# Index lists from six half-precision instructions, attention's last batch in halves, its row statistics in the first steps

## The chip, the cores and the metric

The kernel runs on one core of one Trainium2 chip. The metric is the device time of one launch in microseconds (us), as the median of three runs: 826.29 us before the change (824.8 to 826.83). The profiled execution, from which every row below is taken, was a run of its own and took 823.37 us.

## The reference

The reference takes hidden states x of shape [4, 512, 256] (2048 tokens of 256 values) and computes a macaron block in float32:

```
x = x + 0.5 * moe(layernorm(x))
x = x + attention(layernorm(x), w_qkv, w_o)      # 16 heads of 16, causal, softmax
x = x + 0.5 * moe(layernorm(x))
```

moe is a top-2 mixture of 8 experts with a capacity of C = 640 pairs per expert:

```
probs = softmax(x @ Wg); gate_vals, expert_idx = top_k(probs, 2)
pos   = how many earlier (token, choice) pairs went to the same expert
kept  = pos < C
dispatch_mask[expert, pos] = token                  # the index list
h = relu(x[dispatch_mask] @ w1[e]);  out[token] += gate * (h @ w2[e])
```

The index list is what the change is mostly about: for each expert and each of its 640 places, which token stands there.

## The kernel before, in words

The program has three stages, one after the other, each a block of its own in which the five engines run their own instruction streams and meet by semaphores: `feed_forward` with the tag first, `attention`, and `feed_forward` with the tag second. A block begins when every engine has left the block before it.

**feed_forward.** The 2048 tokens stand as 128 partitions by T = 16 columns. The first stage loads x, transposes it and computes the router's logits on TensorE; in the second stage attention has left logits and moments behind. VectorE then takes the two largest logits of each token, counts with a running sum, and TensorE adds over the partitions (L721, L722), so that each of the K * T = 32 columns of pairs has a position within its expert. The list is built as a sum of 32 outer products. Places are numbered as 128 lanes by LC = 40 tiles (8 experts by 5). For each pair column n, VectorE writes `of_tile[:, n, :]` (40 values: the token's number where the pair's tile is, else 0; L619) and `of_lane[:, n, :]` (128 values: 1 where the pair's lane is; L620), and TensorE adds the product of the two into ps_x (L733), waiting for each pair column by `lane_ready`. After every eighth product it runs 8 products whose result nobody reads (`spin`, L222), and 60 more after the last one. `spin` multiplies a table of ones; its only effect is that TensorE is not idle.

VectorE turns the sum into `gather_now` and `gather_index` (L624, L625). GpSimd waits for the normed rows and the shares to be stored in DRAM (`stored`, written by SyncE from `xn`, which ScalarE fills at L175, and `shares`), then gathers the 5 tiles of expert 0 and the 5 of expert 1 by indirect DMA (L410). TensorE transposes the gathered tiles in three batches of 2, 2 and 1 (L748, with 8 spins between), ScalarE and VectorE split them into a high and a low part (L501, L633, with the split of w2 at L548 between the first and second batch on VectorE), and the loop over the 8 experts begins with the matmul at L765.

GpSimd also fills the constant tables at the start of the first stage (`Constants.fill`, L91 to L95 by iota, `wide_gate` after them), and copies `slot_tile` into `slots` at the start of either stage (L381). VectorE waits for that copy (`slots_made`) before its routing work.

**attention.** Queries, keys and scores are worked in 16 units of 4 heads (4 units per batch). The order of all engines is one list, `PLAN`, made by `step_plan(v)` for v from -5: step v issues the batch work (`rows`, `stacks`, `values_in`), the scores of unit v + 2 (six pieces, S), the keys of unit v (six pieces, N), and so on. `normalize(b)` is in the plan four steps ahead of a batch; on VectorE it computes the row statistics of batch b (L1150 to L1155), on GpSimd the inverse root and the normed rows. Front pieces take turns in two pairs of PSUM banks: a piece waits for whoever reads the piece two before it, for scores VectorE's maximum (L1180). For the last batch, `project` adds the result to x in one instruction (L1218), `turn_x` transposes x (8 transposes, L1393) once `out_ready` is set, ScalarE copies the result (L1122), and `logits` multiplies by the gate (16 matmuls, L1401). At its start TensorE runs 70 spins.

## Time and profile before

| | us |
|---|---|
| median of three runs | 826.29 |
| lowest and highest | 824.8 and 826.83 |
| profiled execution | 823.37 |
| its span on the core | 821.6 |
| TensorE matmul busy in the span | 766.5 (93%) |
| VectorE busy | 434.2 (53%) |
| ScalarE busy | 376.2 (46%) |
| GpSimd busy | 316.8 (39%) |

The span runs from the first to the last instruction of the profile; 1.77 us of the profiled execution lie around it. Busy time of TensorE includes spins, so 93% is not 93% of useful work. The granted clock is the share of full speed (2.4 GHz) at which TensorE was let run; it has the two levels 1.0 (2.4 GHz) and 0.5 (1.2 GHz), and a value between them is a stretch with both. The stages lie at 0 to 294 us (first), 294.7 to 545.7 us (attention) and 545.98 us to the end (second).

### The profile page before, as it was taken

The page shows a single profiled execution, that of the slowest core. Times are in us where ns is not written, and L with a number is a line of the kernel's source. Part 1 is how long each engine was busy: PE and PEld are TensorE (multiplying, and loading weights), DVE is VectorE, ACT ScalarE, POOL GpSimd, SP SyncE. Part 2 cuts the span into 40 slices and gives each one's busy share as a digit, 9 for nine tenths or more (in the row PEclk, how much of TensorE's full clock was granted, in tenths as well). Part 3 has the DMA queues.
Part 4 walks back from the last instruction along what each step waited for, and adds up shares of the span by engine and source line. Part 5 has one row for each costly group of instructions (what it writes and reads, how often), then busy time and mean ns, then how long its engine had stood idle before and what let it go on. Part 6 is the DMA issues. An engine that isn't in the chain of part 4 may idle for free. (4 is left out here: it accounts for less than half of the span.)

```text
span 821.6 us, 16019 instructions
## 1 busy us (share of the span) xinstructions
PE 766.5 (93%) x6176; PEld 675.1 (82%) x6176; DVE 434.2 (53%) x850; ACT 376.2 (46%) x630; POOL 316.8 (39%) x373
## 2 busy tenths in 40 slices
PE   9689999999999987898998989967899999999997
PEld 5579999999999975565665655655899999999997
DVE  5945445534634226767676675456446345444630
ACT  4415545634544301556646556513345445544631
POOL 6073454464424263232232122222644554463133
PEclk9779999999999997899999999986999999999999
DMA  9542553354242154201222010024541553454122
GB/s 305 160 147 74 146 141 93 87 155 126 47 121 27 16 166 154 76 18 72 78 81 106 33 70 11 26 78 126 182 128 41 155 134 82 107 146 117 26 27 25
DMA packets 61862, 80.27 MB, mean 98 GB/s; under 512 B 10916, under 2 KB 48804, under 8 KB 61812
## 3 DMA queue, kind: packets, MB, share of 16 engines
q1 hardware_dynamic: 46452, 60.34, 21.8%
q0 software_dynamic: 15360, 19.23, 12.8%
q8 instruction: 35, 0.57, 0.3%
q14 instruction: 15, 0.12, 0.0%
HBM read 49.62 MB, written 19.01 MB: 84 GB/s over the span
## 5 line engine op out<-in xcount | busy, mean ns | idle before, releaser
L655 DVE SCALAR_TENSOR_TENSOR second_h_lo<-second_ps_h,second_h_hi 128x320 fp32r<-128x320 f32 x128 | 63.0, 492 | 105.2 <-ACT second_h_hi L514 105.2
L655 DVE SCALAR_TENSOR_TENSOR first_h_lo<-first_ps_h,first_h_hi 128x320 fp32r<-128x320 f32 x128 | 62.9, 492 | 104.8 <-ACT first_h_hi L514 104.8
L418 POOL DMA_INDIRECT after_first<-first_scaled,first_add_now x40 | 69.4, 1736 | 117.5 <-ACT first_scaled L507 110.9
L418 POOL DMA_INDIRECT out_dram<-second_scaled,second_add_now x40 | 69.0, 1725 | 117.2 <-ACT second_scaled L507 111.5
L1180 DVE TENSOR_REDUCE at_maxima<-at_ps_front 128x4 f32<-128x512 f32 (+2 forms) x96 | 97.0, 1040 | 21.1 <-PE at_ps_front L1321 20.6
L1052 POOL TENSOR_SCALAR_AFFINE_SELECT at_probs<-at_probs 128x512 f32<-128x512 f32 x64 | 41.3, 658 | 147.0 <-ACT at_probs L1110 147.0
L776 PE MATMUL second_ps_o<-second_w_hi,second_h_hi 128*128 128x256 f32 x320 | 90.9, 284 | 0.0
L776 PE MATMUL first_ps_o<-first_w_hi,first_h_hi 128*128 128x256 f32 x320 | 90.7, 283 | 0.0
L776 PE MATMUL second_ps_o<-second_w_lo,second_h_hi 128*128 128x256 f32 x320 | 89.7, 280 | 0.0
L776 PE MATMUL second_ps_o<-second_w_hi,second_h_lo 128*128 128x256 f32 x320 | 89.7, 280 | 0.0
L776 PE MATMUL first_ps_o<-first_w_lo,first_h_hi 128*128 128x256 f32 x320 | 89.5, 280 | 0.0
L776 PE MATMUL first_ps_o<-first_w_hi,first_h_lo 128*128 128x256 f32 x320 | 89.5, 280 | 0.0
L1110 ACT ACTIVATE at_probs<-at_ps_keys 128x768 f32<-128x768 f32 (+1 forms) x96 | 81.1, 879 | 17.5 <-PE at_ps_keys L1352 17.0
L514 ACT ACTIVATE second_h_hi<-second_ps_h 128x320 fp32r<-128x320 f32 x128 | 56.1, 438 | 60.4 <-PE second_ps_h L765 60.4
L514 ACT ACTIVATE first_h_hi<-first_ps_h 128x320 fp32r<-128x320 f32 x128 | 56.1, 438 | 60.4 <-PE first_ps_h L765 60.4
L765 PE MATMUL first_ps_h<-first_xt_hi,first_w_hi 128*128 128x320 f32 x256 | 59.0, 312 | 2.2 <-DVE first_xt_lo L633 2.2
L776 PEld LDWEIGHTS second_ps_o<-second_w_hi,second_h_lo 128*128 128x128 f32 x320 | 60.9, 190 | 0.0
L776 PEld LDWEIGHTS first_ps_o<-first_w_lo,first_h_hi 128*128 128x128 f32 x320 | 60.8, 190 | 0.0
L776 PEld LDWEIGHTS second_ps_o<-second_w_lo,second_h_hi 128*128 128x128 f32 x320 | 60.8, 190 | 0.0
L776 PEld LDWEIGHTS second_ps_o<-second_w_hi,second_h_hi 128*128 128x128 f32 x320 | 60.7, 190 | 0.0
L776 PEld LDWEIGHTS first_ps_o<-first_w_hi,first_h_hi 128*128 128x128 f32 x320 | 60.7, 190 | 0.0
L776 PEld LDWEIGHTS first_ps_o<-first_w_hi,first_h_lo 128*128 128x128 f32 x320 | 60.7, 190 | 0.0
(297 smaller groups left out, 1763.5 us busy)
## 6 DMA issues: line engine op xcount, KB each, us to landing
first_w_raw<-in_L_ffn_w_dram SPq DMA_DIRECT2D x16, 1024.0 KB, 8.9
second_w_raw<-in_L_ffn_w_dram SPq DMA_DIRECT2D x15, 1024.0 KB, 5.7
at_q_stack<-at_pre_hi SPq DMA_DIRECT2D x12, 256.0 KB, 2.5
at_k_stack<-at_pre_hi SPq DMA_DIRECT2D x12, 256.0 KB, 2.6
x<-_attn_hidden_states_dram SPq DMA_DIRECT2D x4, 512.0 KB, 5.4
after_first<-x SPq DMA_DIRECT2D x4, 512.0 KB, 7.8
normed_rows<-first_xn SPq DMA_DIRECT2D x4, 512.0 KB, 4.6
x<-after_first SPq DMA_DIRECT2D x4, 512.0 KB, 5.6
```

Of the source, the lines that this page charges most:

```text
L418: pool.indirect_dma_start(sum_rows, bass.IndirectOffsetOnAxis(ap=add_now[par][:, s:s + 1], axis=0), scaled[par][:, s, :], None, bounds_che ...
L514: act.activation(h_hi[:, f, a * HALF:(a + 1) * HALF], ps_h[:, f % 2, a, 0:HALF], ACT.Relu).then_inc(h_hi_done, 1)
L655: v.scalar_tensor_tensor(h_lo[:, f, a * HALF:(a + 1) * HALF], ps_h[:, f % 2, a, 0:HALF], 0.0, h_hi[:, f, a * HALF:(a + 1) * HALF].bitcast( ...
L765: last = pe.matmul(ps_h[:, f % 2, a, 0:HALF], w, m, start=(n == 0), stop=(n == len(parts) - 1))
L776: last = pe.matmul(ps_o[:, (par + s) % 2, 0:D], h[:, f, cs], w[par][:, f, :], start=(f == 0 and n == 0), stop=(f == FT - 1 and n == 2))
L1052: pool.affine_select(block_of, block_of, [[0, GROUP], [1, P]], ALU.is_ge, 0.0, base=0, channel_multiplier=-1).then_inc(cleared, 1)
L1110: act.activation(probs[v % 2][:, 2 * p:2 * p + 2, first:end], keys_banks(item)[:, :, 0:end - first], ACT.Exp, scale=float(HD) ** -0.5).the ...
L1180: v_.reduce_max(maxima[v % 2][:, qt, :, pairs[0]:pairs[-1] + 1], banks, AX_X).then_inc(front_v, 1)
```

## The change

1. `of_tile` and `of_lane` are filled by a few large instructions in place of 64 small ones. With `slots` now [128, 40, 32], one instruction compares all 1280 tile entries, one multiplies them by the token numbers into `tokens_of`, and four (`lanes(h)`) compare 1024 lane entries each. All operands are float16, so `in_tile`, `tile_column` and `token1` become float16; `column` keeps its type and a new `tile_column` takes the sum. The innermost index is now the pair column, so a product's weights are `of_lane[:, n // 8, :, n % 8]` (every eighth value of a partition) and its moving side `tokens_of[:, :, n]` (every 32nd).
2. GpSimd writes `slots` by an iota of 1280 entries in either stage, and `lane` by one of 1024; `slot_tile` is gone.
3. TensorE's spins: before the position products 50 (first) or 36 (second) in place of 40; new, 36 or 40 ahead of the list's products; the 3 x 8 among them go; 34 in place of 60 behind them.
4. Attention: `normalize` is split into `statistics` and `normalize`; the statistics of batches 1 to 3 stand in the steps v = -5 to -3. TensorE gets spins in those steps (14 in the first, 4 elsewhere), and 80 in place of 70 at the start.
5. Attention's `project`, `turn_x` and `logits` work in two halves of two row tiles each, with semaphores of their own.
6. Some semaphores are made in the first stage only (`once`); nothing waits on them in the second.

```diff
-        self.lane = sb("lane", [P, P], F16)
-        self.slot_tile = sb("slot_tile", [P, LC])
+        self.lane = sb("lane", [P, P, E], F16)
         self.rank = sb("rank", [P, E])
         self.first_tile = sb("first_tile", [P, E])
-        self.token1 = sb("token1", [P, K, T])
+        self.token1 = sb("token1", [P, K, T], F16)
...
-        pool.iota(self.lane[:], [[1, P]], base=0, channel_multiplier=0, **small).then_inc(self.filled, 1)
-        pool.iota(self.slot_tile[:], [[1, LC]], base=0, channel_multiplier=0, **small).then_inc(self.filled, 1)
+        pool.iota(self.lane[:], [[1, P], [0, E]], base=0, channel_multiplier=0, **small).then_inc(self.filled, 1)
...
-            in_tile = eb("in_tile", [P, K * T])
+            in_tile = eb("in_tile", [P, K * T], F16)
+            tile_column = eb("tile_column", [P, K * T], F16)
             numbers = eb("numbers", [P, LC])
-            slots = eb("slots", [P, LC], F16)
-            of_tile = eb("of_tile", [P, K * T, LC], F16)
-            of_lane = eb("of_lane", [P, K * T, P], F16)
+            slots = eb("slots", [P, LC, K * T], F16)
+            of_tile = eb("of_tile", [P, LC, K * T], F16)
+            tokens_of = eb("tokens_of", [P, LC, K * T], F16)
+            of_lane = eb("of_lane", [P, K * T // E, P, E], F16)
...
-            pool.tensor_copy(slots[:], const.slot_tile[:]).then_inc(slots_made, 1)
+            pool.iota(slots[:], [[1, LC], [0, K * T]], base=0, channel_multiplier=0,
+                      allow_small_or_imprecise_dtypes=True).then_inc(slots_made, 1)
...
-                  v.tensor_tensor(column[:], column[:], tile_no[:], ALU.add))
+                  v.tensor_tensor(tile_column[:], column[:], tile_no[:], ALU.add))
             token = const.token1[:].rearrange("p k t -> p (k t)")
-            for n in range(K * T):
-                v.tensor_scalar(of_tile[:, n, :], slots[:], column[:, n:n + 1], token[:, n:n + 1], ALU.is_equal, ALU.mult)
-                v.tensor_scalar(of_lane[:, n, :], const.lane[:], in_tile[:, n:n + 1], None, ALU.is_equal).then_inc(lane_ready, 1)
+
+            def lanes(h):
+                part = slice(h * PART, (h + 1) * PART)
+                v.tensor_tensor(of_lane[:, h], const.lane[:], in_tile[:, part].unsqueeze(1).broadcast_to([P, P, PART]),
+                                ALU.is_equal).then_inc(lane_ready, 1)
+
+            every = [P, LC, K * T]
+            v.tensor_tensor(of_tile[:], slots[:], tile_column[:].unsqueeze(1).broadcast_to(every), ALU.is_equal).then_inc(chained, 1)
+            chain.count += 1
+            lanes(0)
+            v.wait_ge(chained, chain.count)
+            v.tensor_tensor(tokens_of[:], of_tile[:], token.unsqueeze(1).broadcast_to(every), ALU.mult).then_inc(tokens_ready, 1)
+            for h in range(1, PARTS):
+                lanes(h)
...
-            spin(pe, const, ps_x[:, 1, :], 40)
+            spin(pe, const, ps_x[:, 1, :], 50 if first_phase else 36)
...
+            spin(pe, const, ps_o[:, 0, :], 36 if first_phase else 40)
+            pe.wait_ge(tokens_ready, 1)
             for n in range(K * T):
-                pe.wait_ge(lane_ready, n + 1)
-                last = pe.matmul(ps_x[:, 1, 0:LC], of_lane[:, n, :], of_tile[:, n, :], start=(n == 0), stop=(n == K * T - 1))
-                if n % PART == PART - 1 and n < K * T - 1:
-                    spin(pe, const, ps_o[:, 0, :], 8)
+                if n % PART == 0:
+                    pe.wait_ge(lane_ready, n // PART + 1)
+                last = pe.matmul(ps_x[:, 1, 0:LC], of_lane[:, n // PART, :, n % PART], tokens_of[:, :, n], start=(n == 0),
+                                 stop=(n == K * T - 1))
             last.then_inc(list_made, 1)
-            spin(pe, const, ps_o[:, 0, :], 60)
+            spin(pe, const, ps_o[:, 0, :], 34)
...
-        if v < -1:
-            return work + sum(S, []) + normal
+        busy = [("spin", v, n) for n in range(6)]
+        if v < -2:
+            return work + [("statistics", v - FIRST + 1)] + busy[0:1]
+        if v == -2:
+            return work + [item for n in range(6) for item in S[n] + busy[n:n + 1]] + normal
+        if v == -1:
+            return [S[0][0], S[1][0], busy[1], S[2][0], busy[2], S[3][0], busy[3]] + turns + [S[4][0], busy[4], S[5][0], busy[5]] + work
...
-    PLAN = [("normalize", 0)]
+    PLAN = [("statistics", 0), ("normalize", 0)]
...
+                half = SEQ // 2
+                act.wait_ge(half_turned, b + 1)
+                act.activation(x_t[:, :, 0:half], front_banks(item)[:, 0, :].rearrange("p (k c) -> p k c", k=DK),
+                               ACT.Copy).then_inc(half_kept, 1)
                 act.wait_ge(front_made, FRONT_AT[item] + 1)
-                act.activation(x_t, front_banks(item), ACT.Copy).then_inc(front_a, 1)
+                act.activation(x_t[:, :, half:], front_banks(item)[:, 1, :].rearrange("p (k c) -> p k c", k=DK),
+                               ACT.Copy).then_inc(front_a, 1)
...
+            def normalize(b):
                 if b == 0:
+                    tiles = slice(0, QT)
...
-                v_.tensor_tensor(flat(x[:, tiles, :]), flat(front_banks(item)), flat(x[:, tiles, :]), ALU.add).then_inc(front_v, 1)
+                for half, signal in enumerate((half_added, front_v)):
+                    rows_of = slice(QT * b + 2 * half, QT * b + 2 * half + 2)
+                    v_.tensor_tensor(flat(x[:, rows_of, :]), front_banks(item)[:, half, :], flat(x[:, rows_of, :]),
+                                     ALU.add).then_inc(signal, 1)
...
-                pe.wait_ge(out_ready, b + 1)
-                for k in range(DK):
-                    for j in range(QT):
-                        last = pe.transpose(banks[:, k, j * P:(j + 1) * P], x[:, QT * b + j, k * P:(k + 1) * P], const.identity[:])
+                pe.wait_ge(half_added, b + 1)
+                for j in range(QT):
+                    if j == 2:
+                        last.then_inc(half_turned, 1)
+                        pe.wait_ge(front_v, FRONT_V[FRONT_AT[("project", b)]])
+                    for k in range(DK):
+                        at = (2 * k + j % 2) * P
+                        last = pe.transpose(banks[:, j // 2, at:at + P], x[:, QT * b + j, k * P:(k + 1) * P], const.identity[:])
                 last.then_inc(front_made, 1)
 
             def logits(b):
                 banks = claim_front(("logits", b))
-                pe.wait_ge(front_a, FRONT_A[FRONT_AT[("turn_x", b)]])
+                pe.wait_ge(half_kept, b + 1)
                 for t in range(QT):
+                    if t == 2:
+                        pe.wait_ge(front_a, FRONT_A[FRONT_AT[("turn_x", b)]])
...
+            def filler(v, n):
+                spin(pe, const, ps_keys[:, 0, :], 14 if v == FIRST else 4)
+
             pe.wait_ge(const.ready, 1)
-            spin(pe, const, ps_keys[:, 0, :], 70)
+            spin(pe, const, ps_keys[:, 0, :], 80)
```

## Rows read from the trace of the kernel before

**Rows 1.** Windows: length, busy (x instructions) per engine, clock, DMA share, GB/s.

```profile
320.00:340.00 20.00, 16.26 (x113) 9.95 (x114) 16.70 (x28) 5.56 (x8) 4.53 (x12) 0.60 0.04 15
600.00:700.00 100.00, 100.00 (x783) 99.98 (x782) 47.27 (x67) 48.18 (x85) 48.67 (x43) 1.00 0.45 115
```

**Rows 2.** VectorE timeline: start, busy us, engine, line, tiles, shapes, count.

```profile
14.90 2.29 DVE L544 TENSOR_TENSOR first_w_lo<-first_w_raw,first_w_hi 128x2048 fp32r<-128x2048 f32 x1 [2.20 <-ACT first_w_hi L477]
27.00 0.18 DVE L607 TENSOR_SCALAR first_tile_no<-first_position 128x32 f32<-128x32 f32 x1
29.18 0.29 DVE L619 TENSOR_SCALAR first_of_tile<-first_slots,first_column,token 128x40 f16<-128x40 f16 x1
...
40.62 0.24 DVE L620 TENSOR_SCALAR first_of_lane<-lane,first_in_tile 128x128 f16<-128x128 f16 x1
```

**Rows 3.** Groups by shape, VectorE, 29 to 42 us: busy us, mean ns.

```profile
L620 DVE TENSOR_SCALAR first_of_lane<-lane,first_in_tile 128x128 f16<-128x128 f16 x32 | 7.7, 241 | 0.0
```

**Rows 4.** Timeline of TensorE and GpSimd behind the first list.

```profile
40.96 9.17 PE L222 MATMUL first_ps_o<-ones_wide 128*128 128x256 bf16 x60
42.27 1.24 POOL L410 DMA_INDIRECT first_xg<-normed_rows,first_gather_now  x1 [13.73 <-DVE first_gather_index L625]
...
47.59 0.95 POOL L410 DMA_INDIRECT first_xg<-normed_rows,first_gather_now  x1 [0.31 <-issue]
49.97 0.60 PE L748 MATMUL first_ps_x<-identity,first_xg 128*128 128x128 f32 x4
...
55.20 0.55 PE L765 MATMUL first_ps_h<-first_xt_hi,first_w_hi 128*128 128x320 f32 x2 [2.23 <-DVE first_xt_lo L633]
```

**Rows 5.** DMA issues of two stretches: KB each, us to landing.

```profile
first_xg<-normed_rows,first_gather_now POOLq DMA_INDIRECT x10, 2.8
normed_rows<-second_shares SPq DMA_DIRECT2D x1, 64.0 KB, 4.2
```

**Rows 6.** Timeline of the second stage, several engines.

```profile
545.99 0.22 POOL L381 CAST second_slots<-slot_tile 128x40 f16<-128x40 f32 x1 [15.24 <-POOLq L885]
546.32 0.29 DVE L576 TENSOR_REDUCE second_top<-router_logits 128x16 f32<-128x128 f32 x1 [0.62 <-POOL second_slots L381]
...
560.85 0.51 SPq L369 DMA_DIRECT2D normed_rows<-second_shares  x1
...
569.79 1.10 POOL L410 DMA_INDIRECT second_xg<-normed_rows,second_gather_now  x1 [13.68 <-DVE second_gather_index L625]
...
581.84 0.84 PE L765 MATMUL second_ps_h<-second_xt_hi,first_w_hi 128*128 128x320 f32 x2 [2.23 <-DVE second_xt_lo L633]
```

**Rows 7.** Timeline of the first stage: GpSimd tables, VectorE behind them.

```profile
3.10 0.25 POOL L91 IOTA lane<- 128x128 f16 x1
3.41 0.14 POOL L93 IOTA rank<- 128x8 f32 x1
...
8.25 0.15 POOL L380 MEMSET first_wide_gate<- 128x64 f32 x1 [0.15 <-POOL hide_half_t L117]
8.89 0.17 DVE L558 TENSOR_TENSOR gate<-first_wg,first_ps_x 128x16 f32<-128x16 f32 x1 [0.15 <-PE first_ps_x L699]
```

**Rows 8.** Timeline of the first steps of attention: TensorE, VectorE.

```profile
294.77 7.80 PE L222 MATMUL at_ps_keys<-ones_wide 128*128 128x256 bf16 x70 [0.99 <-PEq L241]
...
306.38 0.72 PE L1266 MATMUL at_ps_front<-at_xt,aw_hi 128*128 128x512 f32 x2 [1.57 <-DVE at_xt L1143]
...
323.57 1.40 DVE L1150 BATCH_NORM_STATS2 stats<-x 128x6 f32<-128x256 f32 x4
```

**Rows 9.** Timeline of the end of attention: VectorE, TensorE, ScalarE.

```profile
539.39 1.22 DVE L1218 TENSOR_TENSOR x<-at_ps_front,x 128x1024 f32<-128x1024 f32 x1 [3.15 <-PE at_ps_front L1266]
540.82 1.06 PE L1393 MATMUL at_ps_front<-identity,x 128*128 128x128 f32 x8 [1.47 <-DVEq L1220]
541.92 1.02 ACT L1122 ACTIVATE at_xn<-at_ps_front 128x1024 f32<-128x1024 f32 x1 [6.40 <-PE at_ps_front L1393]
543.09 2.38 PE L1401 MATMUL at_ps_front<-gate,at_xn 128*128 128x8 f32 x16 [1.21 <-ACT at_xn L1122]
```

More of the change, by code:

```diff
@@ L108, in fill @@
             rows = slice(half * HALF_ROWS, (half + 1) * HALF_ROWS)
-            pool.wait_ge(self.filled, 15 + 6 * half)
+            pool.wait_ge(self.filled, 14 + 6 * half)
             for part in range(2):
@@ L315, in feed_forward, with once @@
         CHUNK = SEQ // P
[L316 to L317 removed]
+        def once(name):
+            return sem(name) if first_phase else None
+        x_loaded = [once(f"x_loaded{c}") for c in range(T // CHUNK)]
+        wg_loaded, x_copied = once("wg_loaded"), once("x_copied")
         normed, stored = [sem(f"normed{c}") for c in range(T // CHUNK)], sem("stored")
[L319 to L320 removed]
+        turned, x_t_ready = once("turned"), once("x_t_ready")
+        gate_mean, gate_centred = once("gate_mean"), once("gate_centred")
         half_ready, shares_ready, gated = sem("half_ready"), sem("shares_ready"), sem("gated")
@@ L1144, in low, with statistics @@
                 last.then_inc(front_v, 1)
-            def normalize(b):
+            def statistics(b):
                 tiles = slice(QT * b, QT * (b + 1))
@@ L1238, in _ @@
                 what, of = item[0], item[1:]
-                if what in ("normalize", "rows", "stacks", "scores", "turns", "outputs", "project", "logits", "weights"):
-                    {"normalize": normalize, "rows": rows, "stacks": stacks, "scores": scores, "turns": turns,
+                if what in ("statistics", "normalize", "rows", "stacks", "scores", "turns", "outputs", "project", "logits", "weights"):
+                    {"statistics": statistics, "normalize": normalize, "rows": rows, "stacks": stacks, "scores": scores, "turns": turns,
                      "outputs": outputs, "project": project, "logits": logits, "weights": weights}[what](*of)
```

20 lines of the change are left out of this document (9 added, 11 removed).

## The prediction

> **What bounds the kernel now.** I read the busy time by stretch first, then each stretch where TensorE is not simply full. The expert loops are: TensorE is busy 100.00 of 100 us at granted clock 1.00 [rows 1]. So whatever moves the first expert matmul (L765) of a stage moves everything behind it by the same amount, and the change is worth what it moves at four places: the first list, attention's first steps, attention's end, the second list.
>
> At a list, VectorE sets the pace. From 29.18 us it alternates L619 and L620, 64 instructions, until 40.86 [rows 2]: 11.7 us, or 0.36 per pair column, and the last product stands with it. Then two waits run side by side. GpSimd issues gathers from 42.27 every 1.33 us, TensorE spins 60 times, 9.17 us from 40.96, and transposes only at 49.97 [rows 4]. A gather lands 2.8 us after its issue [rows 5], so batch one (two tiles) was there at 42.27 + 1.33 + 2.8 = 46.4: the spins hold it up by 3.6 us. From the transposes to L765 it is 55.20 - 49.97 = 5.2 us. Without the spins' delay, L765 would start at the first gather plus 1.33 + 2.8 + 5.2 = 9.4 us.
>
> **First list.** The new instructions have 2 x 1280 + 4 x 1024 entries. No row shows a two-tensor instruction in float16. Upper bound: float32, 2.29 us for 2048 entries, 1.04 ns an entry with 0.16 fixed [rows 2]. Nearest row by type: L620 takes 241 ns for 128 float16 entries against 180 ns for 32 entries of L607 [rows 2, 3], so 0.64 ns an entry. I take that. Successive instructions overlap by some 0.08 us (an L619 and L620 pair lasts 0.53, yet pairs follow each other at 0.36), so an instruction costs 0.90 (1280 entries) or 0.73 (1024): 2 x 0.90 + 4 x 0.73 = 4.7 us in place of 11.7. At the float32 rate it is 7.3 us.
>
> The Trainium skill ("VectorE: DVE Perf Modes", section "The perf-mode tier table") gives a tensor-tensor operation on 16-bit operands twice the float32 rate; 0.52 ns an entry would make it 3.9 us. That is an estimate from the page, 0.8 us below my value, and would help only in the first stage.
>
> TensorE now has eight products behind the last lane instruction. Their weights have a stride of 8 values and their moving side one of 32; no row shows a strided operand. Nearest row from below: a spin at full clock, 7.80 / 70 = 0.11 us [rows 8]; from above: a pair of float32 matmuls in 0.55, 0.275 each [rows 4]. Nothing suggests a gain below 0.11. I take 0.11, since the product has float16 weights like the spin's 16-bit ones. `tokens_of` is ready 2.5 us into the list (0.90 + 0.73 + 0.90); 32 products from there end at 2.5 + 3.5 = 6.0 us, TensorE then being slightly the later one.
>
> Ahead of it, GpSimd's tables get slower: 128 entries take 0.25, 8 take 0.14 [rows 7], 0.92 ns each, so `lane` with 1024 entries costs 0.82 more, less about 0.11 for the table that goes. `wide_gate`, filled from 8.25, is then ready at 9.1, and VectorE's gate work, which ran at 8.89 [rows 7], starts some 0.3 later; TensorE's router follows it. The iota of `slots` there (1.3 us) lies in GpSimd's wait for moments. The 50 spins and the 36 new ones end before VectorE's results come. So the list starts at 29.5, its products end at 35.5, the first gather goes 1.3 later as before (40.96 to 42.27), at 36.8, and L765 starts at 46.2: **9.0 us gained**. The 34 spins, 3.8 us, end before the gathers land. Bounds: 6.7 at the float32 rate, 3.5 at 0.275 a product, 11 where strides are free and the lists twice as fast.
>
> **Second list.** Here another wait is late next. GpSimd may gather only once rows and shares are stored. SyncE issued the shares at 560.85 [rows 6] and they land 4.2 us later [rows 5], at 565.05, hidden before behind the gather's start at 569.79. The stage begins with GpSimd's copy into `slots` (0.22), for which VectorE waits [rows 6]; the iota takes 1.3, 1.1 more, and it stands ahead of GpSimd's inverse roots, which ScalarE's rows, hence the stores, wait for. So the store lands at 566.15. The list, 5.8 us shorter (11.8 down to 6.0), even if it started 1.1 later, would permit a gather at 565.1. The store decides: gather at about 566.85 (0.7 for wait and issue, an estimate within the 1.3 above), L765 at 576.25 instead of 581.84, 5.6 us. TensorE idles some 4 us ahead of the gather's landing and may fall to clock 0.5, where its 16 spins between batches take 0.22 instead of 0.11 each; about 0.6 of their 1.8 us shows. **5.0 us gained**, between 3.5 and 6.5. It is nearly blind to the list's exact speed.
>
> **Attention's first steps.** The statistics at 323.57 (1.40, with two small ones 1.9 us) stand on VectorE between the maxima of units 0 and 1, in the stretch where VectorE is the busiest at 16.70 of 20 us [rows 1, 8]. They move to steps where VectorE waits. That frees 1.9 us. The clock there is 0.60; with the spins TensorE could run this stretch's work at 1.00, which I value at 1.0 us, mainly the row transposes and key products that VectorE does not hide. Against it: 14 spins fit in the 1.57 us idle at 306.38 [rows 8], but the 4 behind `stacks` and the 4 behind `values_in` push the second `stacks` by 0.9, of which 0.5 remains after ScalarE's wait. **2.4 gained.** Bounds: 4 with nothing lost; a loss of 1.4 if all 22 spins run at half clock (22 x 0.22 - 1.57 = 3.3 against 1.9). GpSimd's `normalize` is moved past nothing; it just finds its variance early. Ten more spins at the start run until the first normed row is transposed anyway. The statistics of batches 2 and 3, later in the plan, lie beside full TensorE work: nothing.
>
> **Attention's end.** From 540.82, transposes 1.06, copy 1.02, logits 2.38 follow each other to 545.47, 4.65 us, after one addition of 1.22 [rows 9]. In halves, the second addition ends as before; behind it come half the transposes (0.53), half a copy (0.6) and half the logits (1.2), with 0.3 for three waits: 2.6 us. **2.0 gained**, between 0 (hand-overs eat it) and 2.5. `once` and the earlier batches' halves: an extra ScalarE instruction each beside TensorE work, nothing.
>
> **Sum.** 9.0 + 5.0 + 2.4 + 2.0 = 18.4 us. From the profiled 823.37 that gives 805.0; this run lay 2.9 below the median, so the forecast for a median is 826.29 - 18.4 = **807.9**, its own range 803 to 812.
>
> **Rivals.**
> *Float32 rate.* The large instructions run at 1.04 ns an entry: the first gain is 6.7, in the second stage the list permits a gather 0.45 after the store. Total 15.8: **810.5**. For it: no row shows two float16 tensors. Against: L620's 0.64.
>
> *Strided products.* TensorE reads every eighth weight more slowly, at 0.275 a product: 32 take 8.8 us, the first gather goes at 42.1 and L765 at 51.5 (gain 3.7); the second gather waits for the list, 2.0 later. Total 11.1: **815.2**. The rows neither show nor exclude it. The Trainium skill ("SBUF — State Buffer", section "Door 1: The DMA port swizzle", its note on cachelines) says that accesses that each cross into a new 16-byte line pay a penalty, and eight float16 values are just that line; it gives no price, and no run here shows one yet.
>
> *Slower: the same products at half a microsecond.* Above 0.3 us a product they bound both lists; with c us each, the first gain is 12.4 - 32c, the second 10.8 - 32c, the rest 4.4: it turns at c = 0.43, and at 0.5 gives a loss of 4.4, **830.7**. Against it: twice the slowest nearby price.
>
> *Cold clock.* TensorE's new waits (about 2 us in the first stage, 4 in the second) leave both first experts at clock 0.5 for a further 7 us each; half of it is lost time, 7 us in all: **814.9**. Against: before, too, TensorE waited 2.23 us ahead of L765 in either stage [rows 4, 6].
>
> *Nothing.* The gathers or stores land so much later, when moved nearer to the stores' traffic, that gains cancel: 825 to 828.
>
> **How the numbers follow.** Forecast 0.60, float32 rate 0.13, strided products 0.13, cold clock 0.06, nothing 0.04, slower 0.04. The range leaves out the last two and reaches from all four terms at their better end (11 + 6.5 + 4 + 2.5 = 24 gained) to just beyond the strided case: 802 to 816. Faster by over 0.3% (2.5 us, what a measurement here tells from no change) 0.92, within 0.3% 0.04, slower 0.04.
>
> **What would show it.** Right: the six list instructions last 0.75 to 1.0 us each; the weight loads of the list's products stay near 0.1 us; first gather near 37 us in the first stage and only 3 us nearer its stage's start in the second, right behind the shares' landing; the spins end before the gathers land; no statistics between units 0 and 1; 2.6 us from the last addition to the logits' end. Wrong: products spaced at 0.2 us or more, list instructions above 1.1 us, a gather that starts long after list and store, L765 at clock 0.5 for longer than before.

## The result, and the profile after

The changed kernel takes 806.0 us (median of 4 runs, 805.4 to 807.6) where the kernel before took 826.6 in the same session: ratio 0.977, 95% interval 0.975 to 0.979. The forecast was 807.9. Its profiled run took 805.76 us, with a span of 804.0 and a mean granted clock of 0.981 (before: 823.37, 821.6, 0.96). The 17.6 us between the two spans are cut below at the same milestones in both traces.

| stretch | predicted | before | after | gained |
|---|---|---|---|---|
| start to first expert matmul (L765, now L784) | 9.0 | 55.20 | 47.38 | 7.82 |
| from there to attention's start | 0 | 239.57 | 238.23 | 1.34 |
| attention's start to unit 15's negated maxima | 2.4 | 210.3 | 206.1 | 4.2 |
| from there to the last batch's addition | 0 | 34.3 | 34.4 | -0.1 |
| last addition to the second stage's start | 2.0 | 6.60 | 4.69 | 1.91 |
| second stage's start to the end | 5.0 | 275.6 | 273.2 | 2.45 |

**First list.** VectorE's timeline of the changed kernel (start, busy us, engine, line, tiles, shapes, count), to be held against [rows 2]:

```profile
31.14 0.82 DVE L631 TENSOR_TENSOR first_of_tile<-first_slots,first_tile_column 128x1280 f16<-128x1280 f16 x1
31.89 0.69 DVE L627 TENSOR_TENSOR first_of_lane<-lane,first_in_tile 128x1024 f16<-128x1024 f16 x1
32.49 0.82 DVE L635 TENSOR_TENSOR first_tokens_of<-first_of_tile,token 128x1280 f16<-128x1280 f16 x1
33.23 1.89 DVE L627 TENSOR_TENSOR first_of_lane<-lane,first_in_tile 128x1024 f16<-128x1024 f16 x3
```

Six instructions take 4.0 us, where 64 took 11.7; one of 1280 entries follows its neighbour after 0.74, one of 1024 after 0.60, that is 0.58 ns an entry. But the list starts at 31.14, not 29.18. TensorE and GpSimd behind it, the same view, against [rows 4]:

```profile
33.37 2.59 PE L753 MATMUL first_ps_x<-first_tokens_of,first_of_lane 128*128 128x40 f16 x32 [0.30 <-DVE first_tokens_of L635]
35.78 5.56 PE L220 MATMUL first_ps_o<-ones_wide 128*128 128x256 bf16 x34
41.52 0.63 PE L767 MATMUL first_ps_x<-identity,first_xg 128*128 128x128 f32 x4 [0.17 <-issue]
...
43.96 0.66 PE L767 MATMUL first_ps_x<-identity,first_xg 128*128 128x128 f32 x4 [0.95 <-DMA first_xg<-normed_rows,first_gather_now]
...
45.91 0.44 PE L767 MATMUL first_ps_x<-identity,first_xg 128*128 128x128 f32 x2 [0.42 <-DMA first_xg<-normed_rows,first_gather_now]
47.38 0.56 PE L784 MATMUL first_ps_h<-first_xt_hi,first_w_hi 128*128 128x320 f32 x2 [1.02 <-DVE first_xt_lo L650]
```

```profile
37.11 1.24 POOL L416 DMA_INDIRECT first_xg<-normed_rows,first_gather_now  x1 [6.38 <-DVE first_gather_index L642]
...
42.43 0.95 POOL L416 DMA_INDIRECT first_xg<-normed_rows,first_gather_now  x1 [0.31 <-issue]
```

The 32 products with their strided operands take 2.59 us, 0.081 each. The first batch of transposes starts 0.17 us behind the spins; the second and third wait for the gathers themselves (0.95 and 0.42 us): the fifth gather is issued at 42.43 and its rows are transposed at 45.91. Why the list starts late stands in GpSimd's and VectorE's timelines of the first microseconds, against [rows 7]:

```profile
3.11 1.93 POOL L90 IOTA lane<- 128x1024 f16 x1
...
9.88 0.15 POOL L385 MEMSET first_wide_gate<- 128x64 f32 x1 [0.15 <-POOL hide_half_t L115]
9.98 1.39 POOL L386 IOTA first_slots<- 128x1280 f16 x1
```

```profile
10.14 0.17 DVE L564 TENSOR_TENSOR gate<-first_wg,first_ps_x 128x16 f32<-128x16 f32 x1 [0.67 <-POOL first_wide_gate L385]
10.35 1.05 DVE L565 COPY first_wide_gate<-gate 128x16 f32<-128x16 f32 x1
```

The `lane` table takes 1.93 us instead of 0.25, `wide_gate` is 1.63 later, and the copy into it lasts 1.05 us (0.18 before) beside the next iota.

**Attention.** Windows of the stretch that answers to [rows 1], 25 to 45 us behind attention's start: TensorE's clock (the third number from the right) is 1.00, where it was 0.60.

```profile
310.80:330.80 20.00, 17.35 (x164) 11.19 (x163) 17.70 (x24) 6.39 (x9) 1.28 (x2) 1.00 0.07 25
```

Most of the new spins of this stage stand between the score pieces of units 0 and 1: 4 behind each of eleven pieces, 44 of the 76 (10 stand at the start, 22 in the steps -5 to -3). The description of the change names only the other 32, and leaves out that the order within step -1 is new too. TensorE's groups by shape, 305.5 to 327 us (busy us, mean ns, idle before):

```profile
L220 PE MATMUL at_ps_keys<-ones_wide 128*128 128x256 bf16 x44 | 6.7, 275 | 0.0
```

At its end, last addition to logits, against [rows 9] (VectorE, TensorE and ScalarE in one timeline):

```profile
526.15 1.29 DVE L1253 TENSOR_TENSOR x<-at_ps_front,x 128x512 f32<-128x512 f32 x2 [3.25 <-PE at_ps_front L1302]
...
526.99 1.16 PE L1433 MATMUL at_ps_front<-identity,x 128*128 128x128 f32 x8 [0.87 <-DVE x L1253]
...
527.65 0.60 ACT L1148 ACTIVATE at_xn<-at_ps_front 128x512 f32<-128x512 f32 x1 [5.47 <-PE at_ps_front L1433]
528.19 0.60 ACT L1151 ACTIVATE at_xn<-at_ps_front 128x512 f32<-128x512 f32 x1
...
528.39 1.92 PE L1443 MATMUL at_ps_front<-gate,at_xn 128*128 128x8 f32 x16 [0.24 <-ACT at_xn L1148]
```

From the addition's end to the logits' end it is 2.87 us, where it was 4.86. Part of that is the clock: before, it fell to 0.50 during the last logits. TensorE's windows of the trace before (length, busy, clock, DMA):

```profile
543.00:544.00 1.00, 0.92 (x9) 1.00 0.26 84
544.00:545.00 1.00, 1.00 (x9) 0.69 0.00 0
545.00:546.00 1.00, 0.47 (x3) 0.50 0.00 0
```

The same 16 matmuls take 2.38 us there [rows 9] and 1.92 here, at a clock of 1.00 throughout: 0.46 of the 1.91 in the table is the clock's.

**Second stage.** TensorE behind the list, and GpSimd's first gather, against [rows 6]:

```profile
544.09 2.59 PE L753 MATMUL second_ps_x<-second_tokens_of,second_of_lane 128*128 128x40 f16 x32 [1.72 <-DVE second_tokens_of L635]
546.50 6.30 PE L220 MATMUL second_ps_o<-ones_wide 128*128 128x256 bf16 x34
556.39 1.08 PE L767 MATMUL second_ps_x<-identity,second_xg 128*128 128x128 f32 x4 [3.59 <-issue]
557.27 1.92 PE L220 MATMUL second_ps_o<-ones_wide 128*128 128x256 bf16 x8
559.89 1.12 PE L767 MATMUL second_ps_x<-identity,second_xg 128*128 128x128 f32 x4 [0.70 <-DMA second_xg<-normed_rows,second_gather_now]
...
564.16 0.90 PE L784 MATMUL second_ps_h<-second_xt_hi,first_w_hi 128*128 128x320 f32 x2 [1.03 <-DVE second_xt_lo L650]
```

```profile
530.84 1.40 POOL L386 IOTA second_slots<- 128x1280 f16 x1 [13.44 <-POOLq L909]
...
552.09 1.10 POOL L416 DMA_INDIRECT second_xg<-normed_rows,second_gather_now  x1 [10.86 <-DMA normed_rows<-second_shares]
```

GpSimd waits 10.86 us for the store of the shares. Spins at 0.24 us, transposes of 1.08 and first expert matmuls of 0.90 are rows of a half-speed TensorE.

### The profile page after: what moved, and what is told of

It reads as the page before. It is cut to its first block and busy times, and to the rows that moved or that the text cites. A ratio compares the mean times of both kernels' runs of the same rounds, so it can differ in the third digit from the quotient of the medians.

```text
span 804.0 us, 16028 instructions
## 1 busy us (share of the span) xinstructions
PE 760.0 (95%) x6234; PEld 672.6 (84%) x6234; DVE 420.9 (52%) x738; ACT 376.4 (47%) x634; POOL 321.6 (40%) x372
## 5 line engine op out<-in xcount | busy, mean ns | idle before, releaser
L795 PEld LDWEIGHTS first_ps_o<-first_w_hi,first_h_hi 128*128 128x128 f32 x320 | 60.7, 190 | 0.0
L795 PEld LDWEIGHTS second_ps_o<-second_w_hi,second_h_hi 128*128 128x128 f32 x320 | 60.7, 190 | 0.0
L795 PEld LDWEIGHTS second_ps_o<-second_w_hi,second_h_lo 128*128 128x128 f32 x320 | 60.7, 190 | 0.0
L784 PE MATMUL first_ps_h<-first_xt_hi,first_w_hi 128*128 128x320 f32 x256 | 58.4, 309 | 1.0 <-DVE first_xt_lo L650 1.0
```

Of the source, the lines that this page charges most:

```text
L784: last = pe.matmul(ps_h[:, f % 2, a, 0:HALF], w, m, start=(n == 0), stop=(n == len(parts) - 1))
L795: last = pe.matmul(ps_o[:, (par + s) % 2, 0:D], h[:, f, cs], w[par][:, f, :], start=(f == 0 and n == 0), stop=(f == FT - 1 and n == 2))
```

## The experiments

Times differ by several us between executions of one kernel here, so each reading rests on a stretch of the trace. Each experiment's ratio is its time over that of the kernel before in the same session. The second stage's start is 0.49 us behind VectorE's copy of the last logits, as in the trace after.

**1. The statistics put back.**

```
             return work + busy[0:1]            # without ("statistics", ...)
...
+                if b > 0:
+                    statistics(b)              # in normalize
```

> The changed kernel (806.0 us), with the statistics of batches 1 to 3 put back into normalize, ahead of the normed rows; the filler spins stay. Theory (most of the 3.0 us gained in attention's first steps came from VectorE, which had the statistics between the score maxima of units 0 and 1): the chain of maxima, from attention's block start to unit 1, gets longer by 1.9 to 2.5 us, and the time is 808.0 to 808.5. Rival (the warm TensorE made the gain, VectorE had slack): unit 1's maxima move by under 0.5 us and the time stays at 806.0, within 0.6.

809.4 us; ratio 0.980 (0.976 to 0.983).

**2. No spins in attention's first steps.**

```
-                spin(pe, const, ps_keys[:, 0, :], 14 if v == FIRST else 4)
+                pass
...
-            spin(pe, const, ps_keys[:, 0, :], 80)
+            spin(pe, const, ps_keys[:, 0, :], 70)
```

> The changed kernel (806.0 us), without the spins between attention's first steps, and with 70 spins instead of 80 at its start; the statistics stay in their new place. Theory (the fillers hold the granted clock at 1.00 there, and that is worth about 1 us): the granted clock of the first 40 us of attention falls from 1.00 towards the 0.8 of the kernel before, and the time is 806.7 to 807.5. Rival (the fillers only push the row work back, VectorE sets the pace anyway): 805.5 to 806.3 and no later maxima in unit 1.

811.4 us; 0.983 (0.979 to 0.987). The two belong together. Negated maxima (VectorE, L1223) behind attention's start, us:

| kernel | unit 0 | unit 1 | unit 2 | unit 3 |
|---|---|---|---|---|
| before (neither) | 28.7 | 38.4 | 48.1 | 60.2 |
| spins alone (1) | 29.2 | 40.8 | 49.5 | 61.6 |
| statistics moved alone (2) | 30.5 | 38.8 | 48.6 | 60.7 |
| both (the changed kernel) | 29.3 | 36.4 | 45.1 | 57.2 |

By unit 3 neither half has gained anything: 1.4 and 0.5 us are lost. Both together gain 3.0. Kernel 2 does win what VectorE's theory promised where it promised it (8.3 us from unit 0 to unit 1, before 9.7), but it has lost 1.8 by unit 0: TensorE waits, the clock falls to 0.50 for 3.4 us, and the first row products take 1.22 us in place of 0.73 (after).

```profile
297.55 1.22 PE L1302 MATMUL at_ps_front<-at_xt,aw_hi 128*128 128x512 f32 x2 [1.57 <-DVE at_xt L1173]
```

Windows of 25 to 45 us behind attention's start, first of kernel 1 and then of kernel 2, show what else is missing in either:

```profile
311.40:331.40 20.00, 16.51 (x140) 9.99 (x138) 16.18 (x29) 4.10 (x6) 4.41 (x11) 0.83 0.04 15
```

```profile
311.10:331.10 20.00, 16.68 (x114) 10.52 (x114) 16.52 (x21) 4.99 (x7) 0.00 (x0) 0.58 0.12 47
```

The clock is 0.83 and 0.58. In kernel 1 VectorE's timeline shows the statistics between the units, and then maxima that wait for TensorE:

```profile
315.56 1.40 DVE L1180 BATCH_NORM_STATS2 stats<-x 128x6 f32<-128x256 f32 x4
...
323.90 1.23 DVE L1215 TENSOR_REDUCE at_maxima<-at_ps_front 128x2 f32<-128x1024 f32 x1 [1.83 <-PE at_ps_front L1359]
```

The loss at unit 1 is 4.4 us, where the theory had 1.9 to 2.5: TensorE waits 1.67 us for a maximum that frees a pair of score banks, its clock falls to 0.50 for 6.8 us, and the next scores are late as well. Both theories had half of it, and for kernel 2 the clock was worth more than the 1 us expected.

**3. Attention's end in one piece** (the additions, the turning, its copy and the logits as before).

```
-                for half, signal in enumerate((half_added, front_v)):
...
+                v_.tensor_tensor(flat(x[:, tiles, :]), flat(front_banks(item)), flat(x[:, tiles, :]), ALU.add).then_inc(front_v, 1)
```

> The changed kernel (806.0 us), with the last addition, the turning of x, its copy and the logits in one piece per batch again, as before the change. Theory (the halves overlap the four steps and are worth what the traces show, 1.91 us from the last batch's addition to the second stage's start): that stretch grows back by 1.9 us and the time is 807.9. Rival (the halves save in the tail but cost about as much in the three earlier batches through the extra ScalarE instruction and waits): the tail grows by 1.9, attention before it is shorter by 1 us or more, and the time is 806.0 to 807.0.

812.1 us; 0.982 (0.977 to 0.986). Addition to second stage: 7.77 us, where the halves need 4.69 (the same in seven traces with a clock of 1.00 there; 5.7 and 5.5 in runs 5 and 8, where it fell) and the kernel before needed 6.60. The row of the logits says why it is more than before:

```profile
537.85 3.55 PE L1429 MATMUL at_ps_front<-gate,at_xn 128*128 128x8 f32 x16 [1.20 <-ACT at_xn L1147]
```

3.55 us instead of 2.38 [rows 9] and 1.92 (after): the clock was 0.50. At a clock of 1.00 the piece would need 7.77 - 1.63 = 6.14 us, and the kernel before 6.60 - 0.46 = 6.14 as well (estimates from these three rows): at equal clock the halves are worth 1.45, not 1.91. The rival's price in the earlier batches does not show: units 13 to 15 follow at 11.1 and 10.1 us, with the halves at 9.9 and 10.1 in one trace, 11.1 and 10.1 in another (7). The total, 4.2 above the expected 807.9, has other parts in this trace: the first list starts at 32.79, and from the last maxima to the addition it takes 38.3 us instead of 34.4, at half clock in part.

**4. Small list instructions, few spins.**

```
-            v.tensor_tensor(of_tile[:], slots[:], tile_column[:].unsqueeze(1).broadcast_to(every), ALU.is_equal).then_inc(chained, 1)
...
+            for n in range(K * T):
+                v.tensor_scalar(of_tile[:, n, :], slots[:], tile_column[:, n:n + 1], token[:, n:n + 1], ALU.is_equal, ALU.mult)
+                v.tensor_scalar(of_lane[:, n, :], const.lane[:], in_tile[:, n:n + 1], None, ALU.is_equal).then_inc(lane_ready, 1)
```

> The changed kernel (806.0 us), but each index list is made by 64 small VectorE instructions again, from the small tables of the kernel before; the spins stay as the change has them (36 or 40 ahead of the products, none between batches of the first stage, 34 behind). It separates the list instructions from the spins. Theory (the list's form is worth what the sum says, less the tables' cost): the first list starts 2 us earlier, lasts 11.8 instead of 4.8 us, the first gather is 5.2 us later, near 42.3; in the second stage the slots come 1.1 us sooner and the list, not the store, permits the gather, some 1 to 2 us later than in the changed kernel; 812 to 813.5. Rival (the fewer spins made the gain in the first stage, since 60 spins held the transposes up by 3.6 us): the first expert matmul moves by under 2.5 us, and the time is 807.5 to 809.

815.9 us; 0.987 (0.983 to 0.991), above the expected range, with two falls of the clock in attention that the trace after lacks. First stage, us:

| | before | small, few spins | changed |
|---|---|---|---|
| list's start | 29.18 | 30.41 | 31.14 |
| list's start to first gather | 13.09 | 13.12 | 5.97 |
| first gather to first expert matmul | 12.93 | 10.35 | 10.27 |

The list's form is worth 7.2 us, the spins 2.6, and the later start costs 2.0: together the 7.8 of the result. (In this run the list started late for another reason: VectorE's gate work waited 1.60 us for TensorE.) In the second stage the first gather came 22.9 us behind the start, by the list, as expected; the changed kernel's came at 21.25, by the store.

```profile
562.47 1.10 POOL L415 DMA_INDIRECT second_xg<-normed_rows,second_gather_now  x1 [13.70 <-DVE second_gather_index L631]
```

**5. More spins around the second list.**

```
+            spin(pe, const, ps_o[:, 0, :], 36 if first_phase else 56)
...
+            spin(pe, const, ps_o[:, 0, :], 34 if first_phase else 76)
```

> The changed kernel, in the second stage with 56 spins ahead of the list's products (40) and 76 behind them (34); the first stage is as it was. In the changed kernel TensorE waited 1.73 us for the second list, the granted clock then fell to 0.50 for 6.4 us, and the first expert matmul (L784) came 12.07 us behind the first gather. Theory (the second list's missing 2.5 us are a cold clock: cold spins between the batches, cold transposes): TensorE stays busy, the clock stays at 1.00, L784 comes 9.5 to 10 us behind the first gather, and its first expert runs at full clock: 2.0 to 4 us less from the stage's start to the end. Rival (the landing of the gathers decides, 3.2 to 3.6 us after their issue): L784 stays 11.5 us or more behind the gather, with a warm clock. If the clock falls all the same, the 76 spins take up to 16.7 us, hold the transposes up by some 5 us, and the stage is longer by that.

805.5 us; 0.975 (0.972 to 0.977). The stretches stand in the table behind run 7.

**6. 60 spins behind both lists.**

```
-            spin(pe, const, ps_o[:, 0, :], 34)
+            spin(pe, const, ps_o[:, 0, :], 60)
```

> The changed kernel with 60 spins behind the list's products instead of 34, as the kernel before had, in both stages. Theory (34 spins are too few only where the gathers wait for the stores): in the first stage the spins end near 44.1 us instead of 41.3, the transposes are later by 2.6 us and the first expert matmul by 0.5 to 2.6; in the second stage the spins end at about 24.8 us behind the stage's start, ahead of the landing, the clock is at 1.00 for the transposes and the first expert matmul comes 1.5 to 2.5 us sooner behind the gather. The time is within 2 us of the changed kernel's. Rival (the spins' number does not matter in the first stage, since the third batch's landing decides there): the first stage's expert start moves by under 0.3 us, and only the gain of the second stage is left.

806.4 us; 0.979 (0.974 to 0.983). In the first stage the rival is the nearer: the expert matmul moves by 0.33, of which 0.13 is a later list, where the theory had 0.5 to 2.6. What the stage lost beyond that (1.66 us, a half clock from 48.2 us on) came in run 7 too, where nothing was changed.

**7. The changed kernel again.**

> The changed kernel itself once more, beside the two that follow, to see how far its stretches vary from one execution to the next with the code untouched. Theory (the half-clock stretches fall differently from one execution to the next, and most of what separates the experiments' totals by up to 3 us beside the mechanism tried is that): its times spread over 3 us or more, its trace has the same first list and the same score maxima of units 0 to 3 within 0.3 us, but the stretch from the last negated maxima to the second stage is either near 39.1 or near 40.6 to 41.6 us, and the second stage lasts 270 to 273 us. Rival (each kernel has its own clock pattern): the stretches of the first trace come again within 0.3 us, among them 39.1 and 273.2, and the times lie within 2 us of 806.0.

807.4 us, 805.2 to 810.9; 0.977 (0.975 to 0.980). The theory holds: its list starts at 31.12 and unit 3 comes at 57.1, as in the first trace, but the first expert started on a half clock (1.7 us more to attention's start), the last addition came 1.7 us later behind the maxima, and the second stage lasted 273.7, slightly above the range. Its span is 809.2: 12.4 gained against the profiled run before, where the first trace shows 17.6, with the same code.

The second stage of twelve traces, us, and the time from the issue of the shares' store to its landing:

| kernel | start to first gather | gather to expert matmul | start to end | store |
|---|---|---|---|---|
| before | 23.80 | 12.05 | 275.6 | 4.2 |
| changed | 21.25 | 12.07 | 273.2 | 4.2 |
| changed again (7) | 21.26 | 12.52 | 273.7 | 4.2 |
| same stage, run 1 | 21.25 | 10.83 | 270.0 | 4.2 |
| same stage, run 2 | 22.28 | 10.73 | 270.9 | 5.3 |
| same stage, run 3 | 21.59 | 11.97 | 271.5 | 4.6 |
| same stage, run 9 | 22.65 | 10.68 | 271.2 | 5.6 |
| 56 and 76 spins (5) | 22.88 | 10.29 | 271.1 | 5.8 |
| 60 spins behind (6) | 22.62 | 10.30 | 270.8 | 5.6 |
| tables moved (8) | 19.79 | 12.33 | 270.0 | 4.3 |
| tables moved, 52 and 80 spins (10) | 21.50 | 10.23 | 269.6 | 6.0 |
| the same, spins at attention's end (11) | 20.93 | 10.24 | 269.1 | 5.4 |

With more spins the expert matmul follows the gather after 10.2 to 10.3 us, and starts at full clock; with 34 it follows after 10.7 to 12.5, as the clock falls. That is the theory of run 5 (10.29, where it had 9.5 to 10), though its clock fell at 562.4 all the same, behind a wait of 3.0 us at the spins' end. The first column's spread has its own cause, the last column; what makes the store land late in some traces stays open. It also limits what the table shows of the spins: all four traces with more spins have a late store, and at the same gather (runs 6 and 9) they differ by 0.4 us only. That more spins are worth about 2 us rests on the medians of runs 8 and 10 below, 804.5 and 802.2.

**8. GpSimd's tables elsewhere.**

```
-        pool.iota(self.lane[:], [[1, P], [0, E]], ...)            # out of the constants
+                pool.wait_ge(gate_centred, 1)                      # first stage, behind wide_gate
+                pool.iota(const.lane[:], [[1, P], [0, E]], ...)
...
+            if not first_phase:                                    # behind the request for the exponentials
+                number_slots()
...
-            v.wait_ge(slots_made, 1)
+            v.wait_ge(slots_made, 2 if first_phase else 1)         # now just ahead of the list
```

> The changed kernel with GpSimd's tables elsewhere. First stage: lane's iota waits until VectorE has centred the gate, and stands ahead of the one for slots; VectorE waits for both only just ahead of the list. Second stage: the iota for slots stands behind the request for the exponentials, and VectorE waits for it just ahead of the list. Theory (the first list started 1.96 us later in the changed kernel because of the long iota ahead of wide_gate and a copy into wide_gate that ran 1.05 us beside another iota; the second stage's store is 1.1 us later because of the iota at its start): the copy lasts about 0.2 us, the first list starts at 29.2 to 29.6 and the first gather at 35.2 to 35.6; in the second stage the first gather comes 20.1 us behind the stage's start instead of 21.25. Together 2.5 to 3 us. Rival (the start of the first list hangs on the loads of x and on ScalarE, the second stage's store on rows that ScalarE makes, neither on GpSimd): both milestones stay within 0.3 us.

804.5 us, 803.9 to 804.6; 0.974 (0.972 to 0.976). The theory holds in both stages. Here are VectorE's rows of the first list's start:

```profile
9.16 0.17 DVE L573 COPY first_wide_gate<-gate 128x16 f32<-128x16 f32 x1
...
29.26 0.82 DVE L639 TENSOR_TENSOR first_of_tile<-first_slots,first_tile_column 128x1280 f16<-128x1280 f16 x1
```

The copy without an iota beside it lasts 0.17 us and the list starts at 29.26, 1.88 sooner. In the second stage the gather is 1.46 nearer to the start, and the store still decides:

```profile
552.52 1.10 POOL L424 DMA_INDIRECT second_xg<-normed_rows,second_gather_now  x1 [10.48 <-DMA normed_rows<-second_shares]
```

**9. Spins at attention's end.**

```
+                if v is None:
+                    spin(pe, const, banks[:, 1, :], 6)
...
+                if b == BATCH - 1:
+                    spin(pe, const, banks[:, 0, :], 12)            # 7 and 6 more in the turnings
```

> The changed kernel with 31 more spins at attention's end, 6, 7, 12 and 6 of them into banks that the next step writes anyway: ahead of the last transposition of value sums, of the last turning of heads, of the last projection and of the last turning of x, where TensorE waits 0.8, 0.9, 1.5 and 0.9 us in the changed kernel. From the last negated maxima to the second stage's start it took 39.1 us in the changed kernel, 40.6 to 40.7 with the statistics back or without the fillers, where the clock fell to 0.50 for 3.4 us during the last projection. Theory (that fall follows TensorE's idle stretch and costs about 1.5 us, and the spins prevent it): no half clock between the last value sums and the logits, and 39.1 us or less. Rival (the fall comes whatever TensorE did just before): half clock there all the same, 40.6 us or more, since cold spins add to it.

806.6 us; 0.977 (0.974 to 0.981). 38.8 us in this trace, as the theory said. But two traces without these spins have 39.1 (the changed kernel and run 6), so one trace does not decide.

**10. Tables elsewhere, 52 and 80 spins.**

```
+            spin(pe, const, ps_o[:, 0, :], 36 if first_phase else 52)
...
+            spin(pe, const, ps_o[:, 0, :], 34 if first_phase else 80)
```

> The kernel with GpSimd's tables elsewhere, and in the second stage 52 spins ahead of the list's products and 80 behind them. Theory (the store-gated wait of 9 us is covered by warm spins, and the list starts earlier, so that both gains add up): first gather 19.8 us behind the second stage's start, first expert matmul 10.3 us behind that, 270 us or less from the stage's start to the end, 803 us. Rival (the clock falls in the spins all the same, which then hold the transposes up): the first expert matmul is 12 us or more behind the gather, 805 us or more.

802.2 us, 801.9 to 803.8; 0.973 (0.971 to 0.975). All five runs lie below all of run 7 and of run 8 on the same chip. The gather came at 21.50, not at 19.8, since the store took 6.0 us; the other marks of the theory were met. TensorE in its second stage:

```profile
544.73 10.58 PE L219 MATMUL second_ps_o<-ones_wide 128*128 128x256 bf16 x80
556.31 0.63 PE L775 MATMUL second_ps_x<-identity,second_xg 128*128 128x128 f32 x4 [1.00 <-issue]
...
562.26 0.56 PE L792 MATMUL second_ps_h<-second_xt_hi,first_w_hi 128*128 128x320 f32 x2 [1.02 <-DVE second_xt_lo L658]
```

Transposes and first expert run at full clock, and no spin is late.

**11. The same with the 31 spins at attention's end.**

> The kernel with the tables elsewhere, the 52 and 80 spins in the second stage, and the 31 spins at attention's end. Theory (the three are independent: 1.9 us in the first stage, 1.5 in the second stage's gather, 1.7 by the warm clock there, and about 1.2 on average at attention's end, where six of eight traces without these spins had the half clock and the one with them had not): no half clock in the last projection, 801 to 803 us, 1 us less than without the spins at attention's end. Rival (the clock falls there in some executions with the spins too): 40.6 us or more in that stretch, and no difference to the kernel without them.

801.9 us, 801.4 to 805.7; 0.973 (0.971 to 0.976): no different from run 10. The stretch took 40.5 us, next to the rival's 40.6, but the clock did not fall in the last projection. TensorE's timeline shows where it fell:

```profile
514.94 4.05 PE L1419 MATMUL at_ps_keys<-at_probs,at_v_ones 128*32 128x512 f32 x32
518.93 0.83 PE L219 MATMUL at_ps_keys<-ones_wide 128*128 128x256 bf16 x6
```

The last value sums take 4.05 us, 2.36 in the trace after, ahead of the first added spin. The idle stretch that the spins fill does not cause this fall. There are two places: in the twelve traces of the changed kernel and its variants, the clock fell over the last value sums in four (runs 2, 4, 7 and 11) and over the last projection, behind TensorE's wait of 1.5 us, in five (runs 1, 3, 5, 8 and 10). Both traces with the added spins are free of the second kind; two traces are too few to say that the spins prevent it.

## Why the prediction was right, step by step

- **The first list, 9.0 predicted.** 7.8 at the first expert matmul. The list's speed was undersold: 0.60 and 0.74 us an instruction, not 0.73 and 0.90, and 0.081 a product, not 0.11. The float32 rate, the strided and the half-microsecond products did not come. The estimate from the Trainium skill ("VectorE: DVE Perf Modes", section "The perf-mode tier table") was 3.9 us for the six; the trace has 4.0, where 4.7 was taken. Two terms were mis-sized the other way. The tables: "some 0.3 later" was 1.96. The slope of 0.92 ns an entry, from tables of 8 and 128 entries, gave 1.07 us for `lane` where it took 1.93; the copy beside the other iota cost 0.9 more (run 8). And "first gather plus 9.4" was 10.27, in the first stage as in every warm second stage: the sum let the first batch's landing decide, but five gathers go out 1.3 us apart, and the fifth one's rows are the late ones. Together: the first gather went 0.3 later than forecast, and the expert followed it 0.9 later.
- **The 1.34 us behind the first list** were not in the sum: the kernel before had a half clock in its first expert, the first trace after had none, and runs 6 and 7 had it again. No run shows that an edit made them.
- **The second list, 5.0 predicted.** The limit was named rightly: the store. The gather came 2.55 us nearer to the start, 2.94 predicted. The rest, L765 no more than 9.4 behind the gather, failed: 12.07. Of the 2.5 us missing, 0.4 are the gather's, 0.9 the fifth gather's landing as in the first stage, and 1.2 the clock's: "about 0.6 of their 1.8 us shows" was the mis-sized term, since the cold stretch cost 1.8 (12.07 less the 10.27 of a warm stage). The clock was at 0.50 twice, from 545 to 551 us behind TensorE's wait for the list, and from 555 to 568 behind its wait for the rows, through the transposes and into the first expert. The rival *cold clock* came true in this stage alone: the stage gained 2.45 and 1.9 in the two traces of the changed kernel, 4.1 to 5.6 in runs 1, 2, 3 and 9, which have the same code in this stage. So how much of the term a single execution shows is partly chance.
- **Attention's first steps, 2.4 predicted.** 3.0 by unit 3, so the size was near, but its working was wrong: 1.9 for VectorE plus 1.0 for the clock, less 0.5. Runs 1 and 2 show that the two do not add; each alone loses by unit 3. The working also counted 22 spins of the 66, without the 44 among the scores; run 2 takes out all of them, so what each part is worth is not shown. The further 1.2 us in attention go with a fall of the clock at 435 us that the profiled run before had (12.8 us for that unit, 11.3 after); runs 2 and 3 had it too, so it belongs to no edit.
- **Attention's end, 2.0 predicted.** 1.91, but 1.45 at equal clock (run 3). The overlap came as worked out; the sum took the logits of the row before, 2.38, for their price, and 0.46 of that was a half clock. In the trace after the fall comes 0.2 us behind the stage's start; whether the shorter end escapes it or that is chance, no run separates.
- **The sum.** 18.4 predicted, 17.6 between the profiled spans, 20.5 between the medians of that session, 18.1 between those of run 7's session (825.5 to 807.4). Errors of +1.2 and +2.5 at the lists were covered by 0.6 to 1.8 in attention, 1.3 of clock that no step explains, and 0.5 of clock at attention's end. The time was right by more than its terms deserve.

What stays open: what lets the clock fall over attention's last value sums or its last projection in nine of the twelve traces and in neither place in three; and what makes the store of the shares land 4.2 or up to 6.0 us after its issue.

## What to carry to other kernels

Where an engine's clock hangs on its neighbour's pace, edits do not add: try a pair as a pair, and read a single run's stretches before its total. When many small instructions become few large ones, follow the tables that feed them: here they cost 2.0 of 9.0 us, and moving them behind the first work that waits, with spins to cover the store, gave 5 us more (run 10). Behind a store-gated gather, count the last gather's landing, not the first.

## What was not expected of the hardware

- GpSimd's iota does not go by entries alone: 1024 entries as 128 by 8 took 1.93 us (1.62 at its later place in run 8), 1280 as 40 by 32 took 1.39. What of the shape or the place does it, no run separates.
- VectorE's copy of 16 values a partition took 1.05 us beside such an iota, and ended with it (11.40 and 11.37); alone it took 0.17 (run 8). The Trainium skill ("GPSIMD Engine Reference", section "Specifications") tells of contention where the two engines share an interface to SBUF; these two rows agree with it, and no run separates it from a wait of another kind.
- The list's weight loads got longer, off the path. Weight loads of the list's products, first before, then after (busy us, mean ns of one):

```profile
L733 PEld LDWEIGHTS first_ps_x<-first_of_tile,first_of_lane 128*128 128x128 f16 x32 | 2.9, 113 | 7.4 <-DVE first_of_lane L620 7.0
```

```profile
L753 PEld LDWEIGHTS first_ps_x<-first_tokens_of,first_of_lane 128*128 128x128 f16 x32 | 2.4, 152 | 0.6 <-DVE first_tokens_of L635 0.6
```

The Trainium skill ("SBUF — State Buffer", section "Door 1: The DMA port swizzle") names a penalty for accesses that cross into a new line, as every eighth float16 value does. These rows do not give its size: before, 95 to 96 ns are loads of the first eight products, 0.36 us apart at full clock, and up to 152 ns are loads right behind spins; after, all 32 take 141 to 171 ns and follow each other at 0.07 us. The stride and the close succession came together. What the rows do show is that the products still follow each other at 0.081 us, since successive loads overlap.

- The clock falls where TensorE's rows show no idle time. Each of the thirteen traces has a fall over the same work, the third last batch of value sums, which takes 3.1 to 4.1 us there in place of 2.4. TensorE's windows (length, busy, clock, DMA) of the trace after:

```profile
496.00:498.00 2.00, 2.00 (x14) 0.72 0.02 4
498.00:500.00 2.00, 2.00 (x20) 0.50 0.00 0
```
